# Routed x in quarter rows, turned by VectorE, with GpSimd's scatter ahead of the later gathers

## The reference, cut to what matters

```
x = x + conv_ref(ln_c(x))                 # per-channel gate
t = tokens(x)                             # [2048, 512]
xn = layernorm(t)
logits = xn @ router_w.T
w = sigmoid(max(logits)); e = argmax(logits)
out[token] = w * ((silu(xn @ w1[e]) * (xn @ v1[e])) @ w2[e])
out = out + (silu(xn @ g) * (xn @ u)) @ d # shared
x = t + out
```

## Time and profile before

| | |
|---|---|
| median of 3 runs | 413.93 us (413.44 to 414.0) |
| span of the profiled execution | 411.6 us |
| its own time | not listed apart from the three runs |
| TensorE busy (mean granted clock 0.995) | 385.1 us, 94% |
| VectorE, ScalarE, GpSimd busy | 258.2, 161.2, 134.6 us |
| routed steps, a stretch of 159 us (231 to 390) | TensorE busy for all of it, GpSimd for 69.1 us |

### The profile page before, as it was taken

One profiled execution on the slowest core, in us unless ns is written; L12 is line 12 of the kernel. 1 busy time (PEld: TensorE's weight loads), 2 busy tenths in 40 slices (PEclk: granted clock), 3 DMA queues, 4 the chain that ended last, 5 costly groups with the idle time before them and its releaser, 6 DMA issues.

```text
span 411.6 us, 6789 instructions
## 1 busy us (share of the span) xinstructions
PE 385.1 (94%) x1982; PEld 303.8 (74%) x1986; DVE 258.2 (63%) x475; ACT 161.2 (39%) x274; POOL 134.6 (33%) x186
## 2 busy tenths in 40 slices
PE   5875659999999999999999999999999999999994
PEld 2442238888888788887888888888888888888883
DVE  6997876555857865656875557547375744676322
ACT  3996852223344324211116245153254515354110
POOL 7787811000100100005030245425535442446201
PEclk9998999999999999999999999999999999999999
DMA  8900502011201561140041469726546773752210
GB/s 321 397 2 0 204 1 78 27 51 60 90 30 53 187 247 53 53 153 27 32 133 41 128 217 323 282 98 256 204 134 219 294 258 118 262 182 71 86 37 30
DMA packets 14763, 55.96 MB, mean 136 GB/s; under 512 B 2575, under 2 KB 2575, under 8 KB 11280
## 3 DMA queue, kind: packets, MB, share of 16 engines
q1 hardware_dynamic: 9936, 40.93, 28.0%
q0 software_dynamic: 4800, 14.69, 10.0%
HBM read 43.02 MB, written 13.63 MB: 138 GB/s over the span
## 4 chain that ended last, share of the span: by engine, by line
PE 81%; DVE 7%; ACT 5%; issue 3%; POOL 2%; DMA 1%; DVEq 0%; POOLq 0%; ACTq 0%
PE GU L1255 47%; PE yb L1255 22%; PE th L1247 4%; PE tx L1240 4%; ACT tiles L534 2%; PE th L1284 2%; DVE search_junk L806 1%; ACT scratch L545 1%; ACT scratch L549 1%; DMA x_sb<-x_tok 1%; PE mb L1255 1%; DVE x_sb L864 1%; DVE tiles L862 1%; DVE bn_parts L871 1%; PE mb L1233 0%
## 5 line engine op out<-in xcount | busy, mean ns | idle before, releaser
L1255 PE MATMUL GU<-w_parts,xT 128*128 (+1 forms) x864 | 213.6, 395 | 0.0
L1255 PEld LDWEIGHTS GU<-w_parts,xT 128*128 128x128 f32 x864 | 158.3, 188 | 31.4
L1255 PE MATMUL yb<-w_parts,hT 128*128 (+1 forms) x420 | 102.6, 392 | 0.0
L1255 PEld LDWEIGHTS yb<-w_parts,hT 128*128 128x128 f32 x420 | 77.8, 188 | 15.7
L605 ACT ACTIVATE hT<-th 128x512 fp32r<-128x512 f32 x36 | 21.6, 599 | 170.8 <-PE th L1247 170.8
L472 POOL DMA_INDIRECT out<-x_sb,scatidx x20 | 37.6, 1879 | 92.5 <-DVE x_sb L1098 85.6
L922 DVE TENSOR_TENSOR w_parts<-w_raw,w_parts 128x2048 f32 (+1 forms) x24 | 54.9, 2288 | 7.4 <-issue 7.2
L907 DVE TENSOR_TENSOR hidden<-hidden,GU 128x512 f32<-128x512 f32 x36 | 24.8, 688 | 40.2 <-PE GU L1255 40.1
L522 ACT ACTIVATE w_parts<-w_raw 128x2048 f32 (+1 forms) x24 | 45.2, 1910 | 4.2 <-issue 3.9
L446 POOL TENSOR_TENSOR x_rstd<-x_mv,eps 128x1 f32<-128x1 f32 x16 | 3.0, 190 | 113.4 <-DVE x_mv L874 113.4
L901 DVE TENSOR_TENSOR hT<-th,hT 128x512 fp32r<-128x512 f32 x36 | 24.8, 689 | 23.9 <-ACT hT L605 23.6
(11 more groups left out here) (233 smaller groups left out, 339.8 us busy)
## 6 DMA issues: line engine op xcount, KB each, us to landing
w_raw<-weights SPq DMA_DIRECT2D x27, 1024.0 KB, 5.3
x_sb<-x_tok SPq DMA_DIRECT2D x8, 512.0 KB, 6.5
xn_d<-tiles SPq DMA_DIRECT2D x16, 256.0 KB, 2.0
z_d<-x_sb SPq DMA_DIRECT2D x16, 256.0 KB, 2.0
tiles<-xn_d,tokidx POOLq DMA_INDIRECT x20, 4.7
x_sb<-z_d,tokidx POOLq DMA_INDIRECT x20, 5.5
out<-x_sb,scatidx POOLq DMA_INDIRECT x20, 6.8
conv<-conv_par SPq DMA_DIRECT2D x1, 10.0 KB, 9.0
```

The costliest lines, as they stand in the source:

```text
L1255: last = pe.matmul(dst, left[:, lp, kc, :], wset(q, k, wp, kc), start=(i == 0), stop=(i == 3 * KC - 1))
```

## The change

Four things change together.

1. x of a routed block is gathered in quarters. norm_tile writes a row interleaved, so that channel f * 128 + c lies at c * 4 + f; a quarter of a stored row (512 B) then holds 32 values of c for all four f. Gather j of a block fetches, for partition 32 q + r, quarter q of the token in slot 32 j + r. The indices quadidx are 4 * token + q, dealt over the partitions by four small matmuls with the matrix `dealer` (deal_slots on TensorE, quad_rows on VectorE).
2. VectorE turns a block in one transpose of 32 x 32 squares (turn_x) into `turned` in SBUF. TensorE's transpose_x of routed blocks goes, and so do x_hi and x_lo of them, in whose place turned_hi and turned_lo read `turned`. turn_x stands ahead of h_lo in the step.
3. fetch_x waits for x_turned instead of tx_done.
4. GpSimd issues scatter(b) ahead of the gathers of x(b+4), where scatter(b) came behind the gather of x(b+4).

```diff
+        turned = search_junk[:, 2 * P:2 * P + C]
+        dealer = turned.rearrange("p (j q r) -> p j q r", j=QUADS, q=QUADS)
...
+            xn_quads = xn_d.rearrange("t (q c) -> (t q) c", q=QUADS)
+
             def gather_x(b):
 
-                pool.indirect_dma_start(xg[:, b % RING, :], None, xn_d[:, :], rows(tokidx, b)).then_inc(xg_in[b % RING], 16)
+                for j in range(QUADS):
+                    pool.indirect_dma_start(xg[:, b % RING, j * P:(j + 1) * P], None, xn_quads, rows(quadidx[:, j, :], b)).then_inc(xg_in[b % RING], 16)
...
             def fetch_x(b):
-                pool.wait_ge(tx_done, NT + b - RING + 1)
+                pool.wait_ge(x_turned, b - RING + 1)
                 gather_x(b)
...
                 if c + 1 < NT:
+                    scatter(b)
                     fetch_x(c + 1)
-                    scatter(b)
...
+            def turned_hi(n, slot):
+                act.wait_ge(x_turned, n - (NT - 1))
+                act.activation(xT[:, slot, HI, :, :], turned.rearrange("p (k t) -> p k t", k=KC), ACT.Copy).then_inc(xhi, 1)
...
-                dve.tensor_scalar(tiles[:, u, :], tile_of(x_sb, t), x1_mv[:, u, 0:1], x1_rstd[:, u:u + 1], ALU.subtract, ALU.mult).then_inc(xn_ready, 1)
+                dve.tensor_scalar(interleaved(tiles[:, u, :]), tile_of(x_sb, t).rearrange("p (f c) -> p f c", f=KC),
+                                  x1_mv[:, u, 0:1], x1_rstd[:, u:u + 1], ALU.subtract, ALU.mult).then_inc(xn_ready, 1)
+
+            def turn_x(b, u, count):
+                dve.wait_ge(xg_in[u], count)
+                dve.wait_ge(xlo, b + NT)
+                dve.transpose(out=turned.rearrange("p (f j r) -> p f j r", f=KC, j=QUADS),
+                              in_=xg[:, u, :].rearrange("p (j c f) -> p f j c", j=QUADS, f=KC)).then_inc(x_turned, 1)
+
+            def turned_lo(n, slot):
+                dve.wait_ge(xhi, n + 1)
+                dve.wait_ge(x_turned, n - (NT - 1))
+                dve.tensor_tensor(xT[:, slot, LO, :, :], turned.rearrange("p (k t) -> p k t", k=KC),
+                                  xT[:, slot, HI, :, :].bitcast(F32), ALU.subtract).then_inc(xlo, 1)
...
+                if n == DEALER_AFTER:
+                    note(dve.tensor_copy(dealer, ident[:, :].rearrange("p (j r) -> p j r", j=QUADS).unsqueeze(2).to_broadcast([P, QUADS, QUADS, QROWS])))
...
+            def quad_rows():
+                dve.wait_ge(slots_dealt, 1)
+                dve.tensor_scalar(quadidx[:, :, :], tx[:, 0:QUADS * NB].rearrange("p (j b) -> p j b", j=QUADS), float(QUADS), quad[:, 0:1],
+                                  ALU.mult, ALU.add).then_inc(quads_ready, 1)
...
             def step(b, u, j, base):
+                ahead = (u + 2) % RING
+                turn_x(b + 2, ahead, j * (16 * QUADS) + 16 * QUADS * (base + 1 + (u + 2) // RING))
                 h_lo(b + NT, u % 2)
-                x_lo(b + (NT + 2), u % 2)
+                turned_lo(b + (NT + 2), u % 2)
...
+            def deal_slots():
+                pe.wait_ge(slots_ready, 1)
+                for j in range(QUADS):
+                    last = pe.matmul(tx[:, j * NB:(j + 1) * NB],
+                                     turned[:, j * P:(j + 1) * P],
+                                     slotinfo[:, 0, 0:NB], start=True, stop=True)
+                last.then_inc(slots_dealt, 1)
...
                 transpose_h(n, u % 2)
-
-                pe.wait_ge(xg_in[ahead], j * 16 + 16 * (base + 1 + (u + 2) // RING))
-                transpose_x(n + 2, xg[:, ahead, :])
                 up_product(n + 1, 1 - u % 2, 1 - u % 2, after % 2, after * 3)
```

More of the change, by code:

```diff
@@ L24 @@
 RING = 4
+QUADS, QROWS = 4, 32
+DEALER_AFTER = 7
 SEARCH_FROM, SEARCH_TO = -24.0, 24.0
@@ L130, in program @@
         scatidx = sb("scatidx", [P, NB], U32)
+        quadidx = sb("quadidx", [P, QUADS, NB], U32)
+        quad_i = sb("quad_i", [P, 1], I32)
+        quad = sb("quad", [P, 1])
         rtmp = tiles[:, :, :].rearrange("p a c -> p (a c)")
@@ L226, in program @@
         slots_ready = sem("slots_ready")
+        slots_dealt = sem("slots_dealt")
+        quads_ready = sem("quads_ready")
+        x_turned = sem("x_turned")
         tables = sem("tables")
@@ L267, in spread_rows, with interleaved @@
             return scratch[:, of * P:to * P].rearrange("p (s b r) -> p s b r", s=to - of, b=B)
+        def interleaved(row):
+            return row.rearrange("p (c f) -> p f c", f=KC)
         def tile_of(buf, t):
@@ L481, in _ @@
             pool.wait_ge(tx_done, NT)
+            pool.wait_ge(quads_ready, 1)
             for b in range(RING):
@@ L504, in _ @@
                     continue
+                with pool.If(needed > b):
+                    scatter(b)
                 if c + 1 < NB:
@@ L655, in _ @@
                     keep_logits(t)
-            x_hi(NT, 0)
+            turned_hi(NT, 0)
             for k in (GATE, UP):
@@ L661, in _ @@
             h_hi(NT - 1, 1)
-            x_hi(NT + 1, 1)
+            turned_hi(NT + 1, 1)
             silu_gate(NT, 0)
@@ L676, in step @@
                 h_hi(b + NT, u % 2)
-                x_hi(b + (NT + 2), u % 2)
+                turned_hi(b + (NT + 2), u % 2)
                 silu_gate(b + (NT + 1), 1 - u % 2)
@@ L713, in _ @@
             own(dve.tensor_copy(iota_f[:, :], iota_i[:, :]))
+            own(dve.tensor_scalar(quad_i[:, :], pidx_i[:, 0:1], QROWS.bit_length() - 1, None, ALU.logical_shift_right))
+            own(dve.tensor_copy(quad[:, :], quad_i[:, :]))
             own(dve.tensor_copy(pidx[:, :], pidx_i[:, :]))
@@ L1114, in _ @@
             h_lo(n + 2, 1)
+            quad_rows()
             block_experts()
@@ L1120, in _ @@
             gated(n + 4, 1)
-            x_lo(NT, 0)
+            turn_x(0, 0, 16 * QUADS)
+            turned_lo(NT, 0)
             add_shared(n + 3)
             lo_of(GATE, 1)
+            turn_x(1, 1, 16 * QUADS)
             h_lo(n + 4, 1)
-            x_lo(NT + 1, 1)
+            turned_lo(NT + 1, 1)
             gated(NT, 0)
@@ L1239, in transpose_x @@
                 for k in range(KC):
-                    last = pe.transpose(tx[:, k * P:(k + 1) * P], src[:, k * P:(k + 1) * P], ident[:, :])
+                    last = pe.transpose(tx[:, k * P:(k + 1) * P], interleaved(src)[:, k, :], ident[:, :])
                 last.then_inc(tx_done, 1)
@@ L1307, in _ @@
                 for k in (2 * half, 2 * half + 1):
-                    last = pe.transpose((th, tx)[half][:, k * P:(k + 1) * P], tiles[:, 0, k * P:(k + 1) * P], ident[:, :])
+                    last = pe.transpose((th, tx)[half][:, k * P:(k + 1) * P], interleaved(tiles[:, 0, :])[:, k, :], ident[:, :])
                 last.then_inc(tx_half if half == 0 else tx_done, 1)
@@ L1375, in _ @@
             transpose_h(n + 2, 1)
+            deal_slots()
             up_product(n + 3, 2, 0, 0, 0)
@@ L1380, in _ @@
             up_product(n + 4, 3, 1, 0, 0)
-            pe.wait_ge(xg_in[0], 16)
-            transpose_x(NT, xg[:, 0, :])
             down_product(n + 3, 0, 0, 0)
@@ L1385, in _ @@
             transpose_h(n + 4, 1)
-            pe.wait_ge(xg_in[1], 16)
-            transpose_x(NT + 1, xg[:, 1, :])
             up_product(NT, 0, 0, 1, 3)
@@ L1392, in step @@
                 n = b + NT
-                ahead = (u + 2) % RING
                 at, after = table_entries(pe, b, range(SET_COL, SET2_COL + 1))
```

## The result

The changed kernel takes 429.1 us (426.0 to 434.4), the kernel before 413.9 (413.4 to 414.0): the ratio is 1.0345 with a 95% interval of 1.0309 to 1.0380, so it is **slower by 3.4%**. The forecast was 427, the range 408 to 435. The one run of 434.4 us, over 1.5% above the fastest, is left out of the ratio. The profiled execution took 429.0 us with a span of 427.0; before, the span was 411.6.

The account below looks back on a forecast made before the run. TensorE bounds the kernel before; with the change GpSimd's gathers, held by VectorE's subtractions, delay the down products. Span 411.6 + 12.8 = 424.4, plus 2.3 from span to median, gives 427 us; range 408 to 435 (the forecast's own 415 to 435).

Parts of the forecast that it names:

- A turning at 0.43: TensorE's routed steps: each removed turning of x saves 0.43 us, 8.6 us for 20.
- The gather of a quarter at 0.95: GpSimd: each of four 512 B-row gathers costs 0.95 us, as one of 2 KB rows; bounds 0.6 and 1.1.
- Holds of 19 x 1.5 = 28.5: GpSimd: each of 19 routed-loop L922 subtractions on VectorE holds back a DMA wanting to start, 1.5 us each.
- The gap of 0.83 ahead of a scatter: GpSimd: a scatter starts 0.83 us after the addition ends, part of a block's set of 8.1 us.
- Six pairs of 20.75: Steps 1 to 16: six pairs, GATE step plus DOWN step, of 20.75 us (18.1 before), besides four free steps.
- The transpose at 0.69: VectorE's 32x32 transpose ahead of h_lo takes 0.69 us (bounds 0.55 to 1.4), losing 0.3 in six GATE steps, 1.8.
- Rival 3: VectorE's transpose is the bound: at 1.4 us or more, GATE steps last 10.5 and the time is 432; chance 7%.
- deal_slots at 0.9: TensorE, once before the loop: 0.45 us waiting for tokidx plus four small fp32 matmuls at 0.1, together 0.9.
- norm_tile at +0.3: VectorE before the loop: strided output lengthens norm_tile from 0.54 to at most 0.84 us; only the first is waited for.
- Rival 1 (TensorE stays the bound, 408.3): Gathers prove cheaper or holds fall into GpSimd's gaps, so TensorE stays the bound: faster, 408.3 us; chance 22%.
- Rival 2 (a hold of gathers under way): VectorE's two-SBUF-input work also stops gathers already under way: 54.5 us instead of 28.5, up to 453; chance 6%.
- Rival 4 (the new order does nothing): GpSimd's queue: gathers ahead of the scatter would give the same sum; shares the forecast's time, no chance of its own.

Follow-up runs that it names:

- the run with a short transpose: Changed kernel with the routed loops' L962 reading one SBUF input (stale PSUM for the other) and the transpose covering 128x32 of 128x512: 410.0 us, ratio 0.990.
- the profile without a dip of the clock: Changed kernel with each weight load of experts 3 to 8 in the routed loops moving only its first quarter: 424.7 us, ratio 1.026.
- without holds alone: Changed kernel with lo_of in the routed loops reading a stale PSUM tile in place of one of two SBUF inputs: 417.5 us, ratio 1.007.
- the best version: Changed kernel, gathers ahead of scatter, VectorE's h_lo ahead of turn_x and registers ahead of gated, ScalarE's GATE split ahead of turned_hi: 414.4 us, ratio 1.0012.
- the version with the scatter first: The version of 414.4 us (new orders on GpSimd, VectorE, ScalarE) with scatter(b) put back ahead of the gathers of x: 430.2 us, ratio 1.037.

## Why the prediction was right, and where it was not

**The sign, the size and the main mechanism held.** Four gathers in the place of one, stretched by L922 (now L962), make x late, and h_lo waits behind the transpose; taking the holds away gives 11.6 us. The signs named for it came: a mean step of 9.84 us, gathers over 2 us, transposes that wait for a DMA of x; but the two largest gaps are 4.2 and 3.5 us, not 1 to 2.5. The down product of step 17 was forecast for 404.3 and starts at 406.47 (before 391.51). Steps 1 to 16 were forecast at 157.1 and last 157.5. That agreement is partly chance, as the terms show.

- *A turning at 0.43:* the 0.87 it starts from is misread; the earlier trace rows give 270.56 - 267.04 - 2.72 = 0.80 and so 0.36. Measured, a step without waits is 0.42 shorter (9.07, 8.65), so 0.43 holds by luck.
- *The gather of a quarter at 0.95:* right, 0.944. 512 B rows cost GpSimd what 2 KB rows cost.
- *Holds of 19 x 1.5 = 28.5:* about right. In 235 to 400 us the gathers of x, the z gathers and the scatters take 64.5, 32.5 and 24.0 us for 62, 18 and 16; less 0.94, 0.95 and 1.01 apiece that is 6 + 15 + 8 = 29. About half of it falls on the z gathers. A small part comes from turned_lo, which had no term.
- *The gap of 0.83 ahead of a scatter:* wrong, 0.30 where the scatter comes straight behind another DMA; in 14 of the 20 scatters the wait is for nothing that the profile shows, 5.4 us in all. The 0.83 of the earlier trace rows held the wake-up after a wait. The set is 7.55, not 8.1: at most 0.55 us over 16 sets, or 9 us, in the change's favour.
- *Six pairs of 20.75:* the shape was wrong. GpSimd is busy for 124 of the 170 us from 240 to 410 and did not run without a break. In place of a small loss in every pair there are two large waits, each with a down product at half the clock behind it (1.7 and 2.6 us). The clock had no term. The landing of 2.6 was near the usual 2.3 (from issue to landing 2.4 at the least, median 3.2, so the 2.15 us estimated beside it is below all), but the 5.2 us beside the weights' loads had no term either.
- *The transpose at 0.69:* 1.09, within the bounds of 0.55 to 1.4. Its term of 1.8 us is what was mis-sized: by the run with a short transpose its length costs some 5.6 us once the holds are gone, 4.8 of them in the loop, since it stands ahead of the splits too. Rival 3, which had this as a bound from 1.4, set its point too high.
- *deal_slots at 0.9:* 1.4; the profile has eight matmuls for its four, in 1.07 us, and 0.26 of wait, and the next product starts 1.77 after the turning of hidden (208.89 to 210.66), where it was 0.36. *norm_tile at +0.3 and the strided reads at 0:* norm_tile takes 0.74 (0.546 before), and the two cost 1.4 us together: that turning starts at 207.98 in the profile without a dip of the clock, at 206.62 before. The dip adds 0.9 in the changed kernel's profile. The two turnings saved ahead of the loop are lost again, mostly to a wait of 0.60 for the turned x. Ahead of the loop the forecast had 0.4, and 3.6 it was.
- *Rival 1 (TensorE stays the bound, 408.3):* fell. Only the run without holds and with a short transpose comes near it, at 410.0; without holds alone it is 417.5.
- *Rival 2 (a hold of gathers under way):* fell. The gather starts at 311.52, L962 at 311.54, and the gather keeps its length. Six gathers of that trace begin 0.02 to 0.9 us ahead of an L962; all six take 0.94, and all 24 executions of L962 take 2.28 to 2.30. One such place:

```profile
311.52 0.94 POOL L480 DMA_INDIRECT tiles<-xn_d,quadidx  x1 [0.30 <-issue]
```

```profile
311.54 2.30 DVE L962 TENSOR_TENSOR w_parts<-w_raw,w_parts 128x2048 f32 x1 [1.79 <-ACT w_parts L541]
```

  The Trainium skill, SBUF — State Buffer (section SBUF: two separate sides), gives the shared ports, between a VectorE instruction with two SBUF inputs and a GpSimd one that reads SBUF, to whichever starts first, for its whole length, while the other is blocked; that is not what this rival assumes. By that, L962 would have been stalled here until the gather's end at 312.46 and lasted some 3.2 us; it lasted 2.30. So the trace agrees where VectorE starts first (the gather of 253.21, stretched to 2.85) and not where GpSimd does. The sign that the prediction named for this rival, a first quarter stretched by turned_lo, did not come: the first quarter of 272.29 was under way when turned_lo started at 272.88, and took 0.97. What turned_lo stretches is a gather that starts within it (281.16, 1.32).

- *Rival 4 (the new order does nothing):* wrong. The step of it that failed is "since GpSimd is busy all the time in my forecast, gathers ahead of the scatter would give the same sum". The sum of GpSimd's work is the same, but the scatter waits for an addition and the gathers need not. Put ahead of them it turns VectorE's lateness into late gathers: 8.4 us in the change, 15.7 in the best version, none in the kernel before.

**What stays open.** The runs don't separate how much of the two large waits is the late landing and how much the order, and a short transpose with the holds in place was not tried. Why the version with the scatter first loses more with the better orders than with the change's own is not known: its waits show it, but in both orders the same work of VectorE (h_lo, transpose, turned_lo, gated, the split of GATE) stands ahead of the addition, and no run isolates what differs.

## What to carry to other kernels

In a queue worked in order, an instruction that waits for another engine's latest result should not stand ahead of prefetches that wait for nothing; how much that costs is not seen from the sum of the queue's work, and it may be nothing while the queue has room. When an operation moves from a busy engine to a less busy one, look for what stands behind it there: here 0.42 us saved in each step on TensorE stood against 1.09 us of transposing ahead of h_lo and the splits, and against three more gathers. New orders on three engines made the loop 2.4 us shorter than before, and what the change costs ahead of the loop took that back, to a tie. Two executions with different dips of the clock differ by 1 to 2 us ahead of the loop: compare the same stretch of both before a difference is put down to an edit. A wait of 3.5 to 4.2 us of TensorE should be priced with what follows it, here 1.7 to 2.6 us more at the lower clock.

## What the hardware showed that was not expected

- A GpSimd indirect DMA is stretched where it starts within a VectorE subtraction with two SBUF inputs, and not where the subtraction starts second (0.94 in all six cases above). Short ones do it too: turned_lo from 280.97 (0.69) stretches the gather at 281.16 to 1.32.
- An indirect gather costs GpSimd 0.94 us and 0.30 of gap for 128 rows, at 512 B (the change) as at 2 KB. Four quarters so cost it four times one.
- VectorE's 32x32 transpose of 128x512 fp32 takes 1.09 us, 0.40 more than a tensor_tensor of that shape; 128x32 takes 0.205.
- A strided output makes the fp32 norm_tile 0.74 instead of 0.546.
- In stretches right after TensorE had idled for 3.5 to 4.2 us the mean granted clock was 0.50 to 0.66. It also falls to about 0.50 somewhere between 54 and 68 us in some executions, at different times in each, and in others not at all.
